# x laid on 128 partitions, the second expert weights kept in SBUF, and a new written order

## The reference

```python
pooled = x.reshape(B, C, 14, 16, 14, 16).sum(axis=(3, 5))
h = einsum('bcij,ce->bije', pooled, channel_weights)          # 64 x 196 x 192
qk = (q * 16 ** -0.5) @ k.T                                   # 12 heads of 16
attn = relu(1 + qk + qk ** 2 / 2); attn /= attn.sum(-1)
h = h + (attn @ v) @ w_proj + b_proj                          # q, k, v of layernorm(h)
p = softmax(layernorm(h) @ router_w.T); top 2, scaled to sum 1
h = h + sum_e w_e * (gelu(n @ w1[e] + b1[e]) @ w2[e] + b2[e]) # n = layernorm(h), F = 768
```

## Time and profile before

| | us |
|---|---|
| three runs, median (lowest, highest) | 1551.34 (1547.84, 1552.79) |
| the profiled execution, its time | 1550.52 |
| its span | 1548.7 |
| TensorE, matmuls, busy | 1280.8 (83%) |
| VectorE busy | 1008.8 (65%) |
| ACT busy | 617.3 (40%) |
| POOL busy | 716.1 (46%) |
| granted clock, mean | 0.906 |

### The profile page before, as it was taken

The page is one execution under the profiler, slowest core; times in us unless marked ns, Lnnn a source line. Parts: engine busy times, 40 slices in busy tenths (PEclk is TensorE's granted clock), DMA queues, the critical chain, the costliest instruction groups (busy, mean ns, idle before and its releaser), DMA issues.

```text
span 1548.7 us, 28863 instructions
## 1 busy us (share of the span) xinstructions
PE 1280.8 (83%) x7793; PEld 1131.5 (73%) x7793; DVE 1008.8 (65%) x3793; ACT 617.3 (40%) x1203; POOL 716.1 (46%) x557
## 2 busy tenths in 40 slices
PE   4465457089898989899898989898989999998996
PEld 3455346068787878787787878787878888887885
DVE  1887877457776868586868686777683433455553
ACT  1021221045353545353434343434343544555554
POOL 0004302514747474647474647465646463432332
PEclk9995555589999999899999899999999999999999
DMA  6979679657889898989898989898963666666766
GB/s 159 255 187 246 195 196 238 174 170 187 243 236 249 221 261 215 263 201 266 214 264 219 260 218 264 220 253 229 238 168 87 182 174 139 156 171 177 188 181 179
DMA packets 194052, 323.11 MB, mean 209 GB/s; under 512 B 25337, under 2 KB 158570, under 8 KB 193962
## 3 DMA queue, kind: packets, MB, share of 16 engines
q1 hardware_dynamic: 150858, 280.98, 63.2%
q0 software_dynamic: 43104, 41.25, 16.1%
HBM read 267.20 MB, written 54.95 MB: 208 GB/s over the span
## 4 chain that ended last, share of the span: by engine, by line
PE 56%; DVE 22%; issue 8%; POOL 5%; DMA 4%; ACT 3%; SPq 2%; DVEq 0%; POOLq 0%; ACTq 0%
PE ps L933 16%; PE ps L961 15%; DVE red L1006 8%; PE ps L760 5%; POOL rows_d L589 4%; PE ps L880 4%; PE ps L904 3%; PE ps L905 3%; DMA w1r<-L_ffn_w 3%; PE ps L828 3%; PE ps L869 2%; PE ps L859 2%; PE ps L847 2%; DVE topi L1132 1%; DVE newton L1072 1%
## 5 line engine op out<-in xcount | busy, mean ns | idle before, releaser
L961 PE MATMUL ps<-w2r,hid 128*128 128x192 f32 x2520 | 453.8, 327 | 19.0 <-ACT hid L703 19.0
L600 POOL DMA_INDIRECT result<-ys,ridx x210 | 326.7, 1556 | 279.2 <-ACT ys L736 181.8
L1006 DVE TENSOR_REDUCE red<-xbuf 112x14 f32<-112x448 f32 x768 | 422.1, 608 | 51.0 <-PE ps L828 49.0
L961 PEld LDWEIGHTS ps<-w2r,hid 128*128 128x128 f32 x2520 | 411.8, 190 | 35.1 <-ACT hid L703 24.6
L589 POOL DMA_INDIRECT rows_d<-rows,sloti x256 | 246.6, 963 | 313.9 <-issue 176.3
L703 ACT ACTIVATE hid<-ps,b1s 128x512 f32<-128x512 f32 (+1 forms) x380 | 230.7, 617 | 380.8 <-PE ps L933 268.6
L610 POOL TENSOR_TENSOR w1l<-w1r,w1h 128x768 fp32r<-128x768 f32 x74 | 146.9, 2078 | 218.9 <-ACT w1h L715 218.6
L933 PE MATMUL ps<-xh,w1h 128*128 128x512 f32 (+1 forms) x380 | 173.7, 457 | 28.4 <-ACT hid L703 15.9
L1230 DVE TENSOR_TENSOR xl<-ps,xh 128x512 fp32r<-128x512 f32 (+1 forms) x64 | 38.2, 596 | 211.6 <-ACT xh L722 211.5
L715 ACT CAST w1h<-w1r 128x768 fp32r<-128x768 f32 x128 | 106.1, 829 | 105.9 <-PE ps L933 59.7
L933 PE MATMUL ps<-xh,w1l 128*128 128x512 f32 (+1 forms) x380 | 140.6, 370 | 0.0
(11 more groups left out here) (169 smaller groups left out, 1795.3 us busy)
## 6 DMA issues: line engine op xcount, KB each, us to landing
xbuf<-x SPq DMA_DIRECT2D x128, 1176.0 KB, 9.2
w1r<-L_ffn_w SPq DMA_DIRECT2D x130, 384.0 KB, 4.8
w2r<-L_ffn_w SPq DMA_DIRECT2D x65, 576.0 KB, 6.0
xr<-rows_d SPq DMA_DIRECT2D x42, 402.0 KB, 3.2
result<-h1s SPq DMA_DIRECT2D x32, 294.0 KB
xr<-rows_d SPq DMA_DIRECT2D x23, 201.0 KB, 2.4
rows_d<-rows,sloti POOLq DMA_INDIRECT x256
rows_d<-pad SPq DMA_DIRECT2D x9, 402.0 KB, 5.6
```

The source lines that it names most:

```text
L600: pool.indirect_dma_start(out, bass.IndirectOffsetOnAxis(ap=ridx[:, b, n:n + 1], axis=0), ys[:, b, n, :], None, compute_op=ALU.add).then_i ...
L961: last = mm(yout(g, b, n), hid[:, m % 3, cols], w2r[:, b, m, :], start=False, stop=m == MC - 1 and n % 2 == 1)
L1006: V.tensor_reduce(red[:, k // 2, CH * (k % 2) + c, :], xbuf[:, k % XSLOTS, c, :].rearrange("p (r j w) -> p j r w", r=2, j=G), AX.XY, ALU.a ...
```

## The change

x is laid out anew on the host, like the weights: a partition takes an eighth of a patch (2 rows of 16 pixels) of 16 of the step's 48 image channels, three groups of them. A step has 14 chunks of 672 KB with seven slots; a chunk is two P, each over 672 columns to 21 sums. `S1` takes over `S2`'s TensorE part: `mixg`, prepared in the setup from `mix` with each row eight times, sums the eighths and mixes in six matmuls. ACT's copy and the `rowsel` matmuls go. `K` and its buffers go; all experts' w2 (`w2a`) are loaded in the prologue, two with each `S10`, and `N` takes its slice by a register on TensorE. Setup buffers are placed inside `hid`, `xr` and `prod`, which makes the room. In the setup, P is spread differently, x's first two chunks are issued ahead of the weights and b2 is split earlier. All orders are new. SP's prologue steps are written out instead of looped.

```diff
-CHUNKS = 2 * IPS
-XSLOTS = 4
-CH = C // 2
+CHUNKS = 14
+XSLOTS = 7
+HALVES = 2
+SUMS = NSUM // (CHUNKS * HALVES)
@@
-STEP_ALONE = """P P S1 P S2 S3 P P P P P P P P S4 P P P P S5 P P P P P P P P P P P S6.0 S6.1 S6.2 S6.3 P S7.0 P P S7.1 P P P
-    S8.0 S8.1 P P S8.2 S8.3 S10 R V.0 V.1 P V.2 V.3 S11 P P P S9 P P P P Q0 P P P P Q1 Q2 P Q3 P""".split()
+STEP_ALONE = """S1 S2 P P S3 P P P P P P P P P P P S4 S5 P P P P S6.0 S6.1 S6.2 S6.3 S7.0 P P S7.1 S8.0 S8.1 S8.2 P S8.3 P
+    S10 R V.0 V.1 V.2 P V.3 P P S11 P S9 Q0 Q1 P P Q2 P Q3""".split()
 ORDER = [
-    """P S1 M2 P L J P X0 M3 S2 P W0 N0 P X1 P N1 N2 P N3 K M4 P S3 I M5 S4 P P P P P P N4 N5 W1 P S5""".split(),
-    """M0 P P <A S6.0 S6.1 <Y N0 M1 P M2 X0 M3 S6.2 S6.3 W0 X1 N1 L P P S7.0 P N2 P P W1 N3 M4 M5""".split(),
-    """M0 P S7.1 S8.0 P P <J S8.1 M1 P <N4 <I <N5 <Y P <K P P M2 X0 P S8.2 S8.3 N0 P S10 W0 R N1 N2 L <A M3 X1 M4
-       V.0 S11 V.1 S9 V.2 P P P P Q0 V.3 P W1 P I Q1 M5 N3 N4 N5 K P Q2 J Q3 P""".split(),
-    """M0 <A P <Y P P P P P M1 P P""".split(),
+    """L S1 M2 S2 X0 M3 P J X1 N0 P N1 N2 P S3 S4 P N3 S5 M4 P W0 P M5 P S6.0 Y N4 P N5 S6.1""".split(),
+    """M0 M1 M2 <W1 <I P N0 S6.2 S6.3 N1 X0 N2 P W0 P M3 X1 S7.0 P M4 P S7.1 P S8.0 <A L J S8.1 W1 A S8.2 P M5 P P
+       I N3 S8.3 S10 R Y N4 N5""".split(),
+    """M0 M1 M2 P X0 N0 N1 V.0 P W0 M3 P S11 N2 V.1 P S9 X1 V.2 W1 L Q0 V.3 Q1 Q2 P P M4 M5 I N3 N4 P J P""".split(),
+    """M0 Q3 <A P M1 <Y P <N5 P""".split(),
 ]
 TAIL_ORDER = [
-    """N0 M2 X0 W0 M3 X1 N1 L J M4 M5 W1""".split(),
-    """M0 M1 <N2 <Y M2 <N3 <K <N4 <N5 <I N0 N1 X0 M3 L X1 J M4 N2 W0 W1 M5 <A N3 N4 N5 I""".split(),
-    """M0 <Y <A M1 M2 X0 W0 N0 M3 X1 <K M4 M5 N1 N2 L J K A N3 N4 I W1 N5 Y""".split(),
+    """N0 M2 X0 W0 M3 X1 L J N1 M4 M5 W1""".split(),
+    """M0 M1 <N2 <Y M2 <N3 <N4 <N5 <I N0 N1 X0 M3 L X1 N2 J M4 I W0 W1 M5 <A N3 N4 N5""".split(),
+    """M0 <Y <A M1 M2 X0 W0 N0 M3 X1 N1 M4 M5 N2 L J A N3 N4 I W1 N5 Y""".split(),
     """M0 M1""".split(),
 ]
@@ load_chunk
-                sp.dma_start(xbuf[:, k % XSLOTS],
-                             xv[bass.ds(s * IPS + k // 2, 1), :, CH * (k % 2):CH * (k % 2) + CH]
-                             .rearrange("b p c w -> p (b c) w")).then_inc(d_x[k % XSLOTS], 16)
+                sp.dma_start(xbuf[:, k % XSLOTS].rearrange("p h n w -> p (h n w)"),
+                             x[bass.ds(s * (CHUNKS * 128) + k * 128, 128)]).then_inc(d_x[k % XSLOTS], 16)
@@ SP, S10
+                if isinstance(s, int) and s < PRO:
+                    for e in range(s * NE // PRO, (s + 1) * NE // PRO):
+                        sp.dma_start(w2a[:, e].rearrange("p m f -> p (m f)"), w2[e]).then_inc(d_w2, 16)
@@ TensorE, S1 (the old S1 and S2 go, and ACT's copy pT between them)
                 pe.wait_ge(s_pooled, s * PARTS + PARTS)
-                lhs = red[:].rearrange("p i c j -> p (i c) j")
-                for jj in range(G):
-                    last = mm(ps[0:IPS * C, 0, jj * G:(jj + 1) * G], lhs[:, :, jj], const("rowsel", ROWP),
-                              start=True, stop=True)
...
+                    for g in range(GROUPS):
+                        o = g * NTOK + hf * TOK
+                        last = mm(ps[0:TOK, 1, hf * 96:(hf + 1) * 96], red[:, o:o + TOK], mixg[:, g],
+                                  start=g == 0, stop=g == GROUPS - 1)
                 last.then_inc(s_mix, 1)
@@ TensorE, N
                 if m == 0:
-                    pe.wait_ge(d_w2[b], loads_to(0, 16))
+                    expert[b % 3] = pe.value_load(seli[0:1, b % 3, 0:1], min_val=0, max_val=NE - 1)
+                w = w2a[:, bass.ds(expert[b % 3], 1), m, :].rearrange("p a f -> p (a f)")
...
-                    last = mm(yout(g, b, n), hid[:, m % 3, cols], w2r[:, b, m, :], start=False,
+                    last = mm(yout(g, b, n), hid[:, m % 3, cols], w, start=False,
@@ TensorE, setup, ahead of the logits
+            for g in range(GROUPS):
+                last = mm(ps[:, 7, g * 2 * IPS * C:(g + 1) * 2 * IPS * C], repeat[:, g * 128:(g + 1) * 128], mix,
+                          start=True, stop=True)
@@ VectorE, P
-                V.tensor_reduce(red[:, k // 2, CH * (k % 2) + c, :],
-                                xbuf[:, k % XSLOTS, c, :].rearrange("p (r j w) -> p j r w", r=2, j=G),
-                                AX.XY, ALU.add).then_inc(s_pooled, 1)
+                V.tensor_reduce(red[:, p * SUMS:(p + 1) * SUMS], xbuf[:, k % XSLOTS, h], AX.X,
+                                ALU.add).then_inc(s_pooled, 1)
@@ VectorE, setup: P are issued by pool_first(n): 4 ahead of the weights' wait, 2 behind "router",
@@ 4 behind "b2" (now ahead of "amat"), 8 ahead of the heads
+            left = PARTS - 18
             for h in range(HEADS):
-                for p in range(PARTS * h // HEADS, PARTS * (h + 1) // HEADS):
-                    P(-1, p, first=True)
+                pool_first(left * (h + 1) // HEADS - left * h // HEADS)
```

More of the change, by code:

```diff
@@ L272, in vit_layer, with part_of, view @@
         ys = sb("ys", [128, 3, TP, E])
+        def part_of(t):
+            flat = t.rearrange("p a b -> p (a b)") if len(t.shape) == 3 else t.rearrange("p a b c -> p (a b c)")
+            used = [0]
+            def view(rows, *dims):
+                n = int(np.prod(dims))
+                used[0] += n
+                v = flat[0:rows, used[0] - n:used[0]]
+                names = " ".join("abc"[:len(dims)])
+                return v.rearrange(f"p ({names}) -> p {names}", **{k: d for k, d in zip("abc", dims)})
+            return view
+        in_hid, in_xr = part_of(hid[:]), part_of(xr[:])
+        repeat = in_hid(IPS * C, IPS * C * 8)
+        resT = in_hid(KH, 4, KA)
+        qk = in_hid(HD, 2, HEADS, U)
+        atmp = in_hid(NF, 2, NF)
+        amat = in_hid(U, HEADS, U)
+        afac = in_xr(NF, 2, 2 * NF).rearrange("p a (b f) -> p a b f", b=2)
+        cws, cwc, rts = in_xr(C, E), in_xr(C, E), in_xr(NE, E)
+        b2f = in_xr(NE, 2, E)
+        gram, cwT, rtT = in_xr(C, C + IPS * C), in_xr(KH, 2, U), in_xr(KH, 2, NE)
+        pos = prod[:].rearrange("p t c -> p (t c)")[:, 0:NT * NE]
         bmat = ys[0:U].rearrange("p a n e -> p (a n e)")[:, 0:HEADS * 2 * NF].rearrange("p (h f) -> p h f", h=HEADS)
@@ L287, in vit_layer @@
         d_late = [sem(f"d_late{i}") for i in range(3)]
-        d_w2 = [sem(f"d_w2_{i}") for i in range(3)]
+        d_w2 = sem("d_w2")
         SETUP = {
             "pool": ["zeros", "fills", "pad"],
-            "dve": ["copies", "cwc", "router", "cwT", "rtT", "gram", "wide", "mix", "amat"]
-                   + [f"score{h}" for h in range(HEADS)] + ["score", "b2"],
+            "dve": ["copies", "cwc", "router", "cwT", "rtT", "gram", "wide", "mix", "mixg", "b2", "amat"]
+                   + [f"score{h}" for h in range(HEADS)] + ["score"],
             "act": ["resT", "logits", "values", "qk", "bmat"] + [f"factors{h}" for h in range(HEADS)],
-            "pe": ["turned", "gram", "wide", "blocks", "logits", "values", "qk", "amat", "bmat"]
+            "pe": ["turned", "gram", "wide", "blocks", "mixg", "logits", "values", "qk", "amat", "bmat"]
                   + [f"factors{h}" for h in range(HEADS)],
@@ L525, in S10 @@
                                  h1s[:, hf * IPS:(hf + 1) * IPS, 0:E]).then_inc(d_h1, 16)
-            handlers = {"P": P, "L": L, "J": J, "K": K, "S10": S10}
-            tiles_do(sp, handlers, s=0, with_tiles=False)
-            with sp.Fori(1, PRO) as s:
+            handlers = {"P": P, "L": L, "J": J, "S10": S10}
+            for s in range(PRO):
                 tiles_do(sp, handlers, s=s, with_tiles=False)
@@ L533, in _ @@
                 load_w1(j, j, first=True)
-                load_w2(j, j, first=True)
             with sp.Fori(PRO, STEPS - 2) as s:
@@ L563, in _ @@
                 sp.wait_ge(d_late[buf], 48 * loads)
-                sp.wait_ge(d_w2[buf], 16 * loads)
         @block.gpsimd
@@ L782, in _ @@
                                      start=True, stop=True))
+            set_wait(pe, "dve", "mix")
+            for g in range(GROUPS):
+                last = mm(ps[:, 7, g * 2 * IPS * C:(g + 1) * 2 * IPS * C], repeat[:, g * 128:(g + 1) * 128], mix,
+                          start=True, stop=True)
+            given("pe", "mixg", last)
             set_wait(pe, "dve", "rtT")
@@ L1017, in link, with pool_first @@
                 dve.wait_ge(s_dvs, n_set[0])
+            pooled = iter(range(PARTS))
+            def pool_first(n):
+                for _ in range(n):
+                    P(-1, next(pooled), first=True)
             dve.wait_ge(d_cst, 16)
+            V.tensor_copy(repeat.rearrange("p (k u) -> p k u", u=8),
+                          const("ident", IPS * C)[:, 0:IPS * C].unsqueeze(2).to_broadcast([IPS * C, IPS * C, 8]))
             V.tensor_copy(base[:], const("base"))
```

101 lines of the change are left out of this document (40 added, 61 removed).

## The result

The changed kernel takes 1505.17 us (median), the kernel before beside it 1552.07: ratio 0.970, 95% interval 0.965 to 0.974. So 47 us were gained where 92 were forecast, and the time lies 5 us above the end of the range. The profiled execution took 1497.5 us (span 1495.7), 53 less than that of before; the runs differ more than before (1497.5 to 1509.5), and the slower ones have the lower granted clock (0.915 down to 0.906).

The account below looks back on a forecast made before the run. The prediction took waits to bound the prologue, and TensorE's own work plus one wait for pooling the middle. Setup -14.7, prologue -12.2 and middle -66 sum to -93 us: 1459 us forecast, eight-in-ten range 1438 to 1500.

Parts of the forecast that it names:

- Setup, -14.7: Setup up to the first S1: pooling P spread differently brings S1 from 69.39 to 54.7 us, range -9 to -16.
- Prologue, -12.2: Four steps without expert tiles: three periods shorter by 3.8 us each, to 50.6, the fourth by 0.8; range -4 to -14.
- Middle, -66: Twelve steps with three tiles each: 5.5 us off each after a 0.6 allowance, from 75.6 us; range -36 to -80.
- +0.9: Middle step: S3 and S4 become neighbours, so S4 waits for ACT's 0.8 us copy, costing 0.9 us.
- -3.3: Middle step: TensorE's wait before S1 falls from 4.3 to about 1.0 us, with 10.0 us of VectorE work behind S9.
- ready at 22.0 ... wants it at 22.9: Middle step: GpSimd's low part of w1 ready at 22.0 us in the next step; tile 1's M0 wants it at 22.9.
- w2 in SBUF, 0: Expert tiles: dropping w2's per-tile loads saves nothing, and TensorE's register work for N's operand address is hidden, costing nothing.
- Tail, 0: 27 tiles without steps: the chain through the w1 load is unchanged, so 0 us, range -4 to +6.
- A: Rival, chance 0.15: the wait moves to late GpSimd work, P, S2 or S3, 3 us a step; middle -30, 1494 us.
- B: Rival, chance 0.14: only pooling's saving comes, 4.0 us a middle step, no clock back; -48, 1476 us.
- C: Rival, chance 0.08: TensorE's sequencer binds on register work for N's passes; at 70 ns a pass 1634 us.
- D: Rival, chance 0.07: new layout or resident weights land late, setup and prologue give nothing; 1485 us.

Follow-up runs that it names:

- e15: e11's kernel with x's first two chunks issued behind the small weights and VectorE's first six P later; on a chip with the kernel before at 1740 us: 1722.20 us, 0.989.
- e1: The changed kernel with chunk N3 placed between S3 and S4, and S5 behind M4: 1470.55 us, ratio 0.949.
- e2: The changed kernel with VectorE's S11 two P earlier and the pick L behind two P, away from GpSimd's low part of w1: 1509.12 us, ratio 0.971.
- e3: The changed kernel with the order moves of both e1 and e2: 1467.62 us, ratio 0.947.
- e10: e1 with four of the P that stand last in the step moved ahead of S6.0: 1457.74 us, ratio 0.942.
- e18: e11 with the step's first low part of w1 on VectorE instead of behind GpSimd's scatters and adds: 1437.05 us, ratio 0.929.
- e11: e3 with four of the P that stand last in the step moved ahead of S6.0: 1456.30 us, ratio 0.940.
- e12: e1 with every tile taking expert 0's second weights, so no register work on TensorE (results differ): 1465.84 us, ratio 0.946.
- e13: e1 with w2 loaded anew for each tile into three buffers instead of kept in SBUF: 1464.39 us, ratio 0.945.
- e4: The changed kernel with the middle's order of the kernel before, its 48 P thinned to 28 and w2 loads left out: 1526.36 us, ratio 0.985.
- e7: e11's kernel on a chip where the kernel before takes 1740 us: 1727.68 us, ratio 0.994.
- e6 to e9: The kernels of e10, e11, e12 and e13 on a chip with the kernel before at 1739.6 us: 1727.08, 1727.68, 1722.92 and 1716.09 us.
- e14 to e17: e18's kernel, then e11 with x behind the weights, the old tail order, or S4 directly behind S3, on slow chips: 1727.54, 1722.20, 1726.43, 1778.74 us.

## Why the prediction was wrong, by its own steps

**Prices.** Right: P at 0.76 to 0.77, twelve passes of S1 in 1.2 us at full clock (1.1 taken) and 2.3 at half (2.0), N's 0.1625 us a pass unchanged.

**Setup, -14.7.** Measured -11.5. The heads took the 14.5 us forecast. The time lost lies ahead of them, and the term that was mis-sized is "two x loads are issued ahead of the weights (+0.8 us of issue; 0 to 3)": the weights came 3.4 us later (17.60 for 14.24), e15 gives 2.7 of it back, and the first S1 2.3 sooner. SP's issues of the nine small weights grew, from 8.5 to 10.9 us, and did not only move.

**Prologue, -12.2.** Measured -12.7: periods of 50.2 to 51.0, with a DMA share of 0.71 where 0.94 was forecast; the new layout's packets are 130 thousand for 194 thousand, and that the DMA engines would be nearly full did not come true.

**Middle, -66.** The step that failed: eleven steps gave 29.9 us where 60.5 were forecast. "-1.5" for the clock behind S1 was right in nine steps of eleven: M2 takes 1.18. "+0.9" for S3 and S4 as neighbours was right for the wait, 0.99, and put the clock at nothing. From S4 on the clock falls in seven of eleven steps, in three of them for some 11 us; the long steps have TensorE busy 3 to 5 us more. With S4 parted from S3 (e1) there is no fall at S4, and 25 of the 30.6 us missing here are back. I had priced the gap before S1 with its clock and the new thin stretch with its gap without it.
"-3.3" for the wait before S1 became -1.5: the 10.0 us of VectorE behind S9 were 1.6 longer for the pick beside GpSimd, and S9 itself stood 2.4 later for S11's cast. The Trainium skill (SBUF — State Buffer, Who interferes with whom) says that VectorE and GpSimd share one port pair as an exclusive lock held for a whole instruction; the trace agrees (2.58 us for a cast on 8 columns beside 2.40 of GpSimd). What these stalls cost the step stays open, since e2 and e3 only moved them to other operations: what helped was to take four P from behind S9 (e10), and then GpSimd's queue held the step (e18).
The whole of it, 69.4 us a step, is what e11 comes near (69.8) and e18 passes (68.8). The forecast summed the terms of one queue and let the others meet it: "just hidden", "ready at 22.0 ... wants it at 22.9". That second margin was real and closed as soon as S1 was early.

**w2 in SBUF, 0.** Right within the measurement (e12, e13), with 0 to 5 us against it. For the rule of the Trainium skill (TensorE: Matmul & The Clock Gate, What happens when you issue a matmul) the prediction had estimated 63 us if each pass brought a register operation. The trace has one of 0.046 us per N, six a tile and 378 in all for 2520 matmuls, on the side that loads the weights, and N's pitch stays 0.1625; so what an operation for each pass would cost no run shows. The fixed time per DMA that the Trainium skill gives (DMA: Bandwidth & Descriptors, Anatomy of one DMA) did not fall on P: VectorE's P waited 1.4 us for x in the whole run.

**Tail, 0.** Measured, with the last step, 6.6 us worse than forecast. Nearly all of it is the last step, which brought none of its 5.5 us: the first row load of the tail is issued 92.8 us after the last S1 for 92.6. The same passes up to S9 keep TensorE busy for 62.1 us at a clock of 0.89, in e1 57.3 at 0.97; with e1's order the stretch from the last S1 on is 4.3 us shorter. Behind that load the tail is 0.9 us longer. Three tiles take 0.5 to 0.6 us more there, which goes with the kept w2 (e12, e13), but undoing it in e13 made the stretch no shorter than e1's.

**Rivals.** The time of 1505 us lies nearest A's 1494, but that is luck: A was given 0.15 and is in e4, e10 and e11 as it was written, while in the changed kernel itself it hides behind the late P. B's sum was 1476 with "no clock back"; in the middle the clock did come back behind S1 and went again at S4. C and D did not occur.

## What to carry to other kernels

Price a wait on TensorE twice: its own length, and what the passes behind it cost at the lower clock. A wait of 1 us among thin passes went with 3 to 5 us more of TensorE's time in five steps of eleven here, and a thick chunk put in its place gave most of it back. When the longest wait of a loop goes, write down for each other engine when its result is ready and when it is wanted: a margin under 1 us is the next wait. Judge a rewritten order apart from the edits that it came with; here the edits alone gave 2.9 us in eleven steps. And when an operation is moved out of another engine's way, look for the one that now stands there before reading the result: e2 removed 4 us of collisions by its plan and 0.9 in the trace.

## What the runs showed of the hardware that was not expected

Steps with the same instructions lost none, some or all of the clock behind the same 0.99 us wait: a granted clock of 1.00, 0.86 or 0.57 over 12 us (after), and what decides between them is not settled; e2 had the long fall in six steps of eleven for three by a change on VectorE alone. All 22 stretched operations of VectorE in the middle of after ended within 0.4 us of the end of a low part on GpSimd, and moving two of them put others of 16 to 128 columns in their place. On the chips of e1, e10 and e18 the kernel before took 1548 to 1550 us, on two others 1740: in e7 four of SP's issues took 10 us instead of 2.3 beside GpSimd's scatters, three prologue steps of e6 to e9 and e14 to e17 were up to 10 us longer, and every middle step but the first some 18 to 20. Which chip a run fell on outweighed every change tried. And the value load on SP took 0.27 us where w2 is loaded per tile and 0.44 where it is kept.
